# A decay product in another walking order, weight rounding on another engine, and a reordered drain

## The reference

```
x = x + xattn(layernorm(x), ctx, ctx)               # 16 heads of 8, causal
scores = clip(q @ k_rec.T * scale)                  # 16 heads, 64 x 64 for each batch
scores = scores * decay[q, k];  attn = softmax(scores)
x = x + (attn @ v_rec) @ Wo                         # over layernorm(x)
scale(w) = max(max|w|, 1e-6) / 127;  wq = round(w / scale(w))
x = x + qlinear(gelu(qlinear(layernorm(x), w1, b1)), w2, b2)
```

## Time and profile before

| | us |
|---|---|
| median of 3 runs | 351.15 (349.74 to 351.43) |
| the profiled execution, whole time | 349.26 |
| its span in the profile | 347.5 |
| first attention, about | 15 to 143 |
| second attention, about | 143 to 283.5 |
| drain, about | 283.5 to 301 |
| feed-forward | 301 to 347.5 |

### The profile page before, as it was taken

One profiled execution on the slowest core, in us unless ns is written; L12 is line 12 of the kernel. 1 busy time (PEld: TensorE's weight loads), 2 busy tenths in 40 slices (PEclk: granted clock), 3 DMA queues, 4 the chain that ended last, 5 costly groups with the idle time before them and its releaser, 6 DMA issues.

```text
span 347.5 us, 12656 instructions
## 1 busy us (share of the span) xinstructions
PE 294.8 (85%) x5263; PEld 202.5 (58%) x5264; DVE 263.0 (76%) x526; ACT 252.2 (73%) x554; POOL 251.5 (72%) x170
## 2 busy tenths in 40 slices
PE   4796989999799999999797979799977758376694
PEld 2464657776567767676565656567555547221274
DVE  1596778989788888888686867768768773789766
ACT  3486868585668698897787878799666537899490
POOL 5187749748299997799999999999999980072000
PEclk9899999999899999999999999999999987879559
DMA  8995000000000000000000000000000000000026
GB/s 190 243 208 120 3 2 4 4 2 4 2 3 4 2 2 6 4 2 2 4 3 3 2 2 4 2 3 3 5 2 2 4 1 2 3 0 0 0 62 181
DMA packets 19098, 9.48 MB, mean 27 GB/s; under 512 B 5153, under 2 KB 18786, under 8 KB 19042
## 3 DMA queue, kind: packets, MB, share of 16 engines
q1 hardware_dynamic: 18322, 8.25, 11.2%
q10 hardware_dynamic: 720, 0.43, 0.6%
HBM read 6.57 MB, written 2.10 MB: 25 GB/s over the span
## 4 chain that ended last, share of the span: by engine, by line
PE 38%; POOL 27%; issue 15%; ACT 10%; DVE 6%; DMA 1%; ACTq 0%; POOLq 0%; DVEq 0%
POOL ud L373 21%; PE ps L542 7%; PE ps L527 5%; PE ps L555 5%; ACT arena L810 4%; POOL ud L379 4%; PE ps L561 3%; PE ps L571 3%; PE ps L467 3%; PE ps L617 3%; PE ps L460 2%; PE ps L451 2%; PE ps L636 2%; DMA con<-in_constants 1%; DVE u L925 1%
## 5 line engine op out<-in xcount | busy, mean ns | idle before, releaser
L750 ACT ACTIVATE pt<-ps 128x512 f32<-128x512 f32 x128 | 76.0, 594 | 41.4 <-PE ps L542 41.4
L379 POOL TENSOR_TENSOR u<-u,mx 128x1024 f32<-128x1024 f32 x32 | 61.0, 1909 | 36.1 <-DVE mx L936 36.1
L936 DVE TENSOR_REDUCE mx<-u 128x16 f32<-128x1024 f32 x64 | 77.4, 1210 | 0.1
L373 POOL TENSOR_TENSOR ud<-u,con 128x1024 f32<-128x1024 f32 x31 | 73.2, 2363 | 0.0
L379 POOL TENSOR_TENSOR ud<-ud,mx 128x1024 f32<-128x1024 f32 x30 | 57.1, 1903 | 2.3
L925 DVE SCALAR_TENSOR_TENSOR u<-ps,rs,arena 128x1024 f32<-128x1024 f32 x32 | 41.1, 1283 | 20.0 <-PE ps L527 19.9
L542 PE MATMUL ps<-con,ud 128*128 128x128 f32 x256 | 36.9, 287 | 16.9 <-POOL ud L379 11.9
L527 PE MATMUL ps<-arena,qT 32*64 32x256 f32 x1024 | 44.4, 403 | 6.4 <-ACT arena L743 4.3
L555 PEld LDWEIGHTS ps<-pt,vx 128*32 128x32 f32 x2048 | 32.0, 110 | 28.0 <-ACT pt L750 13.6
L930 DVE TENSOR_SCALAR u<-ps 128x1024 f32<-128x1024 f32 x32 | 39.0, 1218 | 9.1 <-PE ps L527 9.0
L555 PE MATMUL ps<-pt,vx 128*32 128x64 f32 x2048 | 42.4, 223 | 3.0 <-ACT pt L750 2.2
(11 more groups left out here) (139 smaller groups left out, 491.9 us busy)
## 6 DMA issues: line engine op xcount, KB each, us to landing
out<-pt SPq DMA_DIRECT2D x8, 256.0 KB, 2.3
x<-in_x SPq DMA_DIRECT2D x4, 256.0 KB, 3.9
arena<-in_ctx SPq DMA_DIRECT2D x8, 128.0 KB, 4.1
x<-in_x SPq DMA_DIRECT2D x2, 512.0 KB, 6.6
arena<-in_ctx SPq DMA_DIRECT2D x4, 256.0 KB, 6.7
arena<-in_mask_BxS_if SPq DMA_DIRECT2D x2, 256.0 KB, 5.4
arena<-in_mask_BxS_if SPq DMA_DIRECT2D x4, 64.0 KB, 4.2
arena<-in_mask_BxS_if SPq DMA_DIRECT2D x2, 128.0 KB, 4.0
```

Source lines behind the costliest of these rows:

```text
L373: pool.tensor_tensor(dh, uh, decay.unsqueeze(1).to_broadcast([P, H, HALF]), ALU.mult)\
L379: pool.tensor_tensor(uh, uh, mx[:, n % 4].unsqueeze(2).to_broadcast([P, H, HALF]), ALU.subtract)\
L750: act.activation(pt[:, n % 2, 4 * half:4 * half + 4].rearrange("p h n -> p (h n)"), ps[:, bank, :], ACT.Exp).then_inc(s["emptied"], 1)
L936: dve.tensor_reduce(mx[:, n % 4], by_head(u[:, n % UB]), AX.X, ALU.max)\
```

## The change

Three parts.

1. **The decay product.** L373 is given the same three tensors with their dimensions in another order: keys outside, heads inside. The instruction then steps through `u` and `ud` in steps of 64 elements (256 bytes), in runs of 16, and the table value stays the same within a run.
2. **The weights.** The four rounding instructions go from POOL (turns 18 to 21) to ACT (turns 20 to 23). On the way there DVE's L853 and L857 disappear: POOL makes the diagonal, with the factor 1/127, in turn 15; the lower bound 1e-6 is a 129th element of the row that DVE reduces. The pieces `wb` and `w1` move from turns 15 and 24 to 17 and 26, and the reciprocal from turn 16 to 18. DVE has three small `memset`s more at the start.
3. **The drain.** In turn 64 PE does `values` and `project` ahead of `to_keys` (before, `to_keys` came first in turns 64 and 65), and ACT's instructions follow that order. Group 6 is normalised by DVE in place of ACT, groups 4 and 6 come one turn earlier, and DVE takes the variance of the last tile in turn 67, not 68.

```
-APPLY3 = (49, 51, 57, 59, 64, 65, 67, 69)
+APPLY3 = (49, 51, 57, 59, 63, 64, 66, 69)
+BY_ACT = 6
-    for kind, n in (("f1", 8), ("f2", 12), ("f3", 16), ("wr", 13), ("wb", 15), ("w1", 24), ("w2", 28)):
+    for kind, n in (("f1", 8), ("f2", 12), ("f3", 16), ("wr", 13), ("wb", 17), ("w1", 26), ("w2", 28)):
...
-        order += to_keys + project if turn >= NS else project + to_keys
+        order += to_keys + project if turn > NS else project + to_keys
...
+                if n == 15:
+                    pool.wait_ge(s["wrow_max"], 1)
+                    pool.tensor_scalar(wmax2[:, 1:3], ident[0:2, 0:2], wmax2[:, 0:1], 1.0 / QP, ALU.mult, ALU.mult)\
+                        .then_inc(s["wdiag"], 1)
...
-                        pool.tensor_tensor(dh, uh, decay.unsqueeze(1).to_broadcast([P, H, HALF]), ALU.mult)\
+                        pool.tensor_tensor(dh.rearrange("p h k -> p k h"), uh.rearrange("p h k -> p k h"),
+                                           decay.unsqueeze(2).to_broadcast([P, HALF, H]), ALU.mult)\
                             .then_inc(s["decayed"], 1)
...
-                if NS <= n < NS + LAG_T:
+                if n == NS + 1:
                     to_keys(n - LAG_T, 0)
                     to_keys(n - LAG_T, 1)
                 if 0 <= n - LAG_PV < NS:
                     values(n - LAG_PV)
                 if 0 <= n - LAG_ADD < NS:
                     project(n - LAG_ADD)
-                if LAG_T <= n < NS:
+                if LAG_T <= n <= NS:
                     to_keys(n - LAG_T, 0)
                     to_keys(n - LAG_T, 1)
...
+            def weights(n):
+                if n == 20:
+                    act.wait_ge(s["wscale"], 1)
+                    act.activation(w1r[:, :, :], w1r[:, :, :], ACT.Identity, bias=cst[:, 1:2], scale=scal[:, 6:7])\
+                        .then_inc(s["w1r_done"], 1)
+                if n == 21:
+                    act.activation(w2r[:, :], w2r[:, :], ACT.Identity, bias=cst[:, 1:2], scale=scal[:, 7:8])\
+                        .then_inc(s["w1r_done"], 1)
+                if n == 22:
+                    act.wait_ge(s["w1r_done"], 1)
+                    act.activation(w1q[:, :, :], w1r[:, :, :], ACT.Identity, bias=cst[:, 4:5]).then_inc(s["wq_done"], 1)
+                if n == 23:
+                    act.wait_ge(s["w1r_done"], 2)
+                    act.activation(w2q[:, :, :].rearrange("o c p -> o p c"),
+                                   w2r[:, :].rearrange("o (p c) -> o p c", c=FC), ACT.Identity, bias=cst[:, 4:5])\
+                        .then_inc(s["wq_done"], 1)
...
-                    dve.tensor_scalar(wmax2[:, 1:3], ident[0:2, 0:2], wmax2[:, 0:1], None, ALU.mult)\
-                        .then_inc(s["wdiag"], 1)
-                if n == 16:
+                if n == 18:
                     dve.wait_ge(s["emptied"], gets_empty(("wb", 0)))
-                    dve.tensor_scalar(scal[:, 4:6], scal[:, 2:4], MIN_RANGE, 1.0 / QP, ALU.max, ALU.mult)\
-                        .then_inc(s["wscale"], 1)
...
-            def last_norm():
+            def last_norm(g):
-                dve.wait_ge(RS[2], len(BATCH[2]))
+                dve.wait_ge(RS[2], batch_of(2, GT * g))
                 dve.wait_ge(s["filled"], gets_empty(("x3", g - 2)))
+                dve.wait_ge(s["amax_done"], g - 1)
...
-                    if 0 <= n - lag - 1 < NT:
+                    if 0 <= n - lag - 1 < NT - (k == 2):
                         variance(k, n - lag - 1)
+                    if k == 2 and n - lag == NT - 1:
+                        variance(k, NT - 1)
```

More of the change, by code:

```diff
@@ L98, in ring_plan @@
                 pieces[n].append((kind, j))
-    for kind, n in (("f1", 8), ("f2", 12), ("f3", 16), ("wr", 13), ("wb", 15), ("w1", 24), ("w2", 28)):
+    for kind, n in (("f1", 8), ("f2", 12), ("f3", 16), ("wr", 13), ("wb", 17), ("w1", 26), ("w2", 28)):
         pieces[n].append((kind, 0))
     for g in range(NG):
-        pieces[APPLY3[g] + 2 if g < 7 else APPLY3[g]].append(("x3", g))
+        pieces[APPLY3[g] + 2 if g < BY_ACT else APPLY3[g]].append(("x3", g))
     order = []
@@ L229, in batch_of @@
             return 1 + next(m for m, (t0, n) in enumerate(BATCH[k]) if t0 <= tile < t0 + n)
-        NMRS = [(turn + 1, k, m) for k, ms in ((1, range(POOLED, NG)), (2, range(4))) for m, turn in enumerate(ROOT_TURN[k])
+        NMRS = [(turn + 1, k, m) for k, ms in ((1, range(POOLED, NG)), (2, range(3))) for m, turn in enumerate(ROOT_TURN[k])
                 if m in ms]
@@ L770, in _ @@
                 there, den = 0 <= n - LAG_T < NS, 0 <= n - LAG_PV < NS
-                if there and n >= NS:
+                if there and n > NS:
                     exponent(n - LAG_T, 0)
@@ L775, in _ @@
                     log_den(n - LAG_PV)
-                if there and n < NS:
+                if there and n <= NS:
                     exponent(n - LAG_T, 0)
@@ L785, in _ @@
                             root(k, m)
+                weights(n)
                 for g, turn in enumerate(APPLY_TURN):
@@ L789, in _ @@
                 for g, turn in enumerate(APPLY3):
-                    if g < NG - 1 and turn <= n <= turn + 1:
+                    if g < BY_ACT and turn <= n <= turn + 1:
                         normalise3(g, n - turn)
@@ L823, in _ @@
             dve.memset(cst[:, 0:1], EPS)
+            dve.memset(wrow[:, P:P + 1], MIN_RANGE)
             dve.memset(cst[:, 2:3], 0.0).then_inc(s["cst_set"], 1)
+            dve.memset(cst[:, 1:2], ROUND)
+            dve.memset(cst[:, 4:5], -ROUND)
             dve.memset(cst[:, 3:4], ROUND16).then_inc(s["cst_set"], 1)
@@ L888, in decay_last @@
                     .then_inc(s["decayed_dve"], 1)
-            def last_norm():
-                g = NG - 1
-                dve.wait_ge(RS[2], len(BATCH[2]))
+            def last_norm(g):
+                dve.wait_ge(RS[2], batch_of(2, GT * g))
                 dve.wait_ge(s["filled"], gets_empty(("x3", g - 2)))
-                for t in range(GT * g, NT):
+                dve.wait_ge(s["amax_done"], g - 1)
+                for t in range(GT * g, GT * g + GT):
                     last = dve.tensor_scalar(xn3[:, g % 2, t % GT], x[:, t], mv[:, 2, t, 0:1], rs[:, 2, t:t + 1],
```

38 lines of the change are left out of this document (10 added, 28 removed).

## The result

| | before | after |
|---|---|---|
| median | 350.44 us (348.04 to 351.43, 4 runs) | 353.38 us (351.8 to 354.25, 4 runs) |
| profiled execution, whole and span | 349.26, 347.5 | 352.81, 351.0 |

The ratio is 1.0106, 95% interval 1.0061 to 1.015: the change makes the kernel about 1% slower. The forecast was 331.5 us.

A forecast was written before the change was run, and what follows sets the result against it. POOL was taken to bound the second attention, PE the first. Decay product -12.5, weights -4.0, rounding on ACT +1.0 and drain -4.0 summed to -19.5 us, giving 331.5 us; range for 8 in 10, 326 to 366.

The forecast's parts named there:

- The L355 row: POOL's one strided instruction, 512 bf16 elements written 256 bytes apart, 3.380 us; kept as the worst case, a product of 5.64.
- rival A: Decay product: the read of `u` pays for its step, product 2.82 us, 358 us in all; chance 0.22.
- the deciding point: Decay product at 2.59 us, 0.23 us longer, where its loss eats the other parts' 7.0 us.
- Rival B: Decay product: the write pays too, as L355 did; product 3.77 to 5.64 us, 388 to 446 us; chance 0.18.
- rival C: Decay product: held operand's gain and step's price cancel at 2.36 us, other parts' -7.0 remain, 344 us; chance 0.10.
- the +1.0 of the sum: Four weight rounding instructions moved to ACT, 3.3 us of work, put +1.0 us on the path, between 0 and 3.3.
- the order of turn 64: Drain: `values` and `project` go ahead of the transposes, filling PE's wait; up to 2.0 us gained.
- The drop of the clock in the gap: Drain: PE's clock, 0.54 from 283.5 to 286.8 us, kept up by work in the gap; some 0.9 us gained.

The follow-up runs named there:

- all but the order: The changed kernel with the decay product back in the old order: 346.58 us, ratio 0.9937 to the kernel before.
- The ten forms: One kernel, executed once, with ten forms of the decay product in rotation over turns 32 to 61; only each form's time was read, 1.903 to 3.043 us.
- weights only: The kernel before with the weights' part, plus DVE's maximum of group 6 ahead of `last_norm`: 346.92 us, ratio 0.9932.
- order only: The kernel before with the decay product in the new walking order and nothing else: 357.99 us, ratio 1.0228.
- group 6 on ACT: The changed kernel with the old product order, the shift term ahead of POOL's last product, and group 6 normalised by ACT: 343.66 us, ratio 0.984.
- weights and turn 64: The kernel before with the weights' part and, of the drain's part, only the order in turn 64: 345.41 us, ratio 0.9875.
- keys outside in u: The kernel before with DVE clipping into `u` keys outside, so the product steps only in its output: 354.01 us, ratio 1.0119.

## Why the prediction was wrong

**The step that failed** is the choice in part 1: "So I take the subtraction as the row that the product is nearest to". The product took 2.576 us, not 1.90. Part 1 was -12.5 us in the sum and measured +6.5, 19 us of the 22 that the forecast was off. The held operand was priced rightly (0.46); the steps were priced at nothing, and cost 0.65 with a write that was almost free and a read that was not. The L355 row, set aside there, was no measure either: its 3.65 ns an element are some 40 times what the output's step costs in f32 (0.087 us for 1024). Which of its two differences, the two-byte elements or the runs of four, makes it so dear was not tested.

The range for 8 in 10, 326 to 366 us, holds the 353.38, but by rival A's share of it (352 to 366, chance 0.22) and not by the forecast's own (326 to 338). Its sums were also a little loose: 329.8 + 1.9 is 331.7, and the terms named for 326 and 338 give 327 and 337. None of this bears on the outcome.

**Rival A** had the mechanism, the read pays for its step, and the deciding point; its price was too high, 0.92 us for the step against 0.57 for the read and 0.09 for the write: a product of 2.59 us was to leave the time unchanged. The product came to 2.58, and the kernel still lost 1%, since parts 2 and 3 were sized at -7.0 and together were worth -2.8 us by the medians (all but the order, 346.58 for 349.39). Rival B, a write as dear as L355's, falls with 0.087 us for the output's step, and rival C, gain and price that cancel, was nearest in its sum: the two came within 0.21 us of each other.

The Trainium skill ("GPSIMD Engine Reference", "Performance pitfalls for Q7 kernels") put the edge at a step of over 8 bytes. The ten forms agree: nothing at 8 bytes, 0.52 us at 16 (input and output together). The size of the price, which the prediction turned into an estimated 0.85 us for 1024 elements, was 0.57. The rule that was set down as showing in no row was the one that decided.

**Part 2** held. L853 and L857 stood for POOL, and without them turn 17 takes 4.57 us; in "weights only" the first product comes 3.4 us earlier, forecast -3.0. Turn 17 gave back 3.46 us, which is the forecast 3.8 less the 0.31 of `wb`, whose move into it was left out of the sum. Turn 15 gave 0.87: the same 0.31, and 0.56 for L853, which the prediction put at 0.2 with 0.6 as the most. By the trace of the changed kernel 4.3 us came back up to turn 19 (counted from turn 13), and 1.1 was given up again on ACT up to turn 31: the +1.0 of the sum. One of ACT's four instructions was mis-sized: L768 took 2.60 us and not 0.82. The same write at its 256-byte steps stood at 3.380 us on POOL in the prediction's own rows. The +1.0 came out right all the same, in part by luck: it was chosen between 0 and 3.3 with 3.3 us of work on ACT in view, and there were 4.95.

**Part 3** failed, -4.0 forecast and +0.4 measured in the changed kernel's drain, +1.1 alone, and 0.6 more at the clock of "order only". "Each step can be lost to the next engine in so short a chain" named the danger but put no price on it. Two new waits appeared, 2.98 us of ACT for the shift term and 2.08 us of PE for group 6. The prediction read that group 6 would be four more instructions on DVE "where it has idle time", and not who stands behind them. Removing the first and moving the second was not enough, since ACT's queue then held the last group; with group 6 on ACT 21.2 us were reached, of the 4.0 forecast 2.6 less than before and 2.0 less than "order only" at the same clock. Of its terms, the order of turn 64 was put at up to 2.0 us and brought about 1. The drop of the clock in the gap didn't go away for good either: in the changed kernel the granted clock was 0.50 from 288 to 291 us. And a piece that the sum didn't name, DVE's maximum of group 6 ahead of `last_norm`, cost an estimated 1.4 us in "weights only" and "weights and turn 64".

What stays open: the last column. In the nine kernels of the table that round the weights on ACT the stretch from the first GELU to the end is 39.8 to 41.6 us, in the four others 42.5 to 44.2. It goes with TensorE's granted clock, which falls to 0.50 between 14.7 and 18.0 us behind the first GELU in all of them and comes back at different times. Before, with the first GELU at 304.97 us, and then weights only, with it at 302.21:

```profile
330.00:335.00 5.00, 5.00 (x33) 3.42 (x32) 3.37 (x6) 5.00 (x3) 0.00 (x0) 0.50 0.23 67
335.00:340.00 5.00, 4.91 (x50) 3.98 (x48) 3.16 (x5) 4.27 (x3) 0.00 (x0) 0.67 0.31 87
```

```profile
330.00:335.00 5.00, 4.63 (x51) 3.35 (x49) 4.73 (x7) 5.00 (x3) 0.00 (x0) 0.90 0.40 108
335.00:340.00 5.00, 4.23 (x66) 3.58 (x64) 4.67 (x8) 2.68 (x2) 0.00 (x0) 1.00 0.71 194
```

Counted from the first GELU, the clock is back at 1.00 after 26.9 to 29.3 us in the nine kernels of the table with the rounding on ACT, and after 33.4 to 36.6 in the four others. The ten forms ran with the rounding on ACT too, and there it was back after 35.0 us and the stretch took 42.3; so where the weights are rounded is not the whole of it. Why the clock comes back at another time was not found, and some of the ratio of each kernel lies in it.

## What to carry to other kernels

Count what each operand pays, not what one saves: on POOL a held operand is worth 0.46 us for 1024 f32 elements, and a first input that steps by 256 bytes costs 0.57. A layout that suits one engine is paid by the one that writes it or reads it next: here 1.4 us of DVE for 0.34 of POOL. And a wait removed from a drain is worth nothing until it's known what stands behind it in the next engine's queue; look at each landmark, not only at the wait.

## What the runs showed that I had not expected

- POOL: stepping in the output is almost free in f32 (0.087 us for 1024 elements 256 bytes apart), stepping in the input is not (0.565), and the two prices add up within the spread of 0.08 us. The 31 products that step in the output alone, in the kernel before with keys outside in u, give the same 2.018 us.
- DVE pays for steps of 64 bytes on either side: 0.70 us for 1024 f32 elements written, 0.73 read.
- ACT pays for bf16 values written 256 bytes apart: 2.60 us for 512, for 0.74 in order. That is 1.86 us more; POOL paid 1.87 for the same.
- POOL's small instructions wait for DVE as DVE's did for POOL: 8 elements took 1.26 and 1.02 us while DVE ran instructions with two SBUF inputs, 0.23 and 0.21 where DVE ran none of these (at 278.25 us it took a maximum, which has one input).
